# First graph layer of a four-layer graph transformer: x also loaded transposed, the layer-norm scale applied behind the projection, and the degrees split between two engines

## The reference, cut to what matters

```python
x = x + gnn0(layernorm(x), adj)      # sim = tanh(adj*adj) where adj > 0, top 350 of a row kept
                                     # h2 = tanh(layernorm(x) @ W_proj + b_proj)
                                     # feat = relu(new_adj @ (h2 @ W_gcn) + b_gcn)
x = x + moe0(layernorm(x))           # 8 experts, top 2, 128 -> 256 -> 128
x = x + gnn1(layernorm(x), adj)      # deg = row sums of adj + I; elu(D^-1/2 (adj+I) D^-1/2 x w)
x = x + block1(layernorm(x))         # attention and a second mixture of 8 experts
```

## Time and profile before

| what | value |
|---|---|
| median of 3 runs | 573.38 us (573.22 to 575.09) |
| the profiled execution's own time | 571.83 us |
| its span in the trace | 570.1 us |
| outside the span | 1.7 us |
| PE busy | 487.1 us, 85% |
| DVE busy | 427.9 us, 75% |
| ACT busy | 314.2 us, 55% |
| POOL busy | 252.3 us, 44% |

### The profile page before, as it was taken

One profiled execution on the slowest core, in us unless ns is written; L12 is line 12 of the kernel. 1 busy time (PEld: TensorE's weight loads), 2 busy tenths in 40 slices (PEclk: granted clock), 3 DMA queues, 4 the chain that ended last, 5 costly groups with the idle time before them and its releaser, 6 DMA issues.

```text
span 570.1 us, 11302 instructions
## 1 busy us (share of the span) xinstructions
PE 487.1 (85%) x3819; PEld 275.4 (48%) x3819; DVE 427.9 (75%) x1065; ACT 314.2 (55%) x522; POOL 252.3 (44%) x275
## 2 busy tenths in 40 slices
PE   1999995879999979998867778889989987898990
PEld 1533333557777745454432233233343226797990
DVE  6897966878999992565778679879977614866674
ACT  0687796966999900120113544456639654466770
POOL 3000002522444440110146189789946575377663
PEclk9999998989999999999957689999999996899996
DMA  8999975200115925011023443200040395869985
GB/s 293 400 422 423 421 274 178 93 1 22 30 28 203 409 58 115 0 42 28 15 75 99 122 118 104 90 2 1 0 143 20 135 356 160 250 182 361 399 299 186
DMA packets 39570, 93.43 MB, mean 164 GB/s; under 512 B 7488, under 2 KB 24944, under 8 KB 35168
## 3 DMA queue, kind: packets, MB, share of 16 engines
q1 hardware_dynamic: 35072, 86.96, 43.4%
q0 software_dynamic: 2272, 4.69, 2.3%
q10 hardware_dynamic: 2176, 1.13, 0.7%
HBM read 69.39 MB, written 21.00 MB: 159 GB/s over the span
## 4 chain that ended last, share of the span: by engine, by line
PE 54%; DVE 20%; DMA 9%; ACT 6%; issue 6%; SPq 3%; POOL 2%; POOLq 0%; DVEq 0%; ACTq 0%
PE ps L1586 9%; DVE A L2393 8%; PE ps L1763 8%; PE ps L1497 7%; PE ps L1514 6%; PE ps L1401 5%; PE ps L1755 3%; DMA R<-in_adj_in 3%; PE ps L1664 3%; DMA A<-w_split 2%; PE ps L1867 2%; PE ps L1611 2%; SPq L812 1%; PE ps L1381 1%; DMA slots_in<-R,A 1%
## 5 line engine op out<-in xcount | busy, mean ns | idle before, releaser
L2393 DVE TENSOR_REDUCE A<-ps 128x1 f32<-128x512 f32 (+3 forms) x160 | 86.1, 601 | 12.3 <-PE ps L1664 11.5
L1302 ACT ACTIVATE A<-ps 128x1024 f32<-128x1024 f32 (+3 forms) x80 | 68.4, 893 | 38.4 <-PE ps L1755 38.2
L1007 POOL TENSOR_TENSOR G<-G,A 128x1024 f32<-128x1024 f32 (+3 forms) x40 | 73.7, 1876 | 8.3 <-ACT A L1302 8.2
L1664 PE MATMUL ps<-A 96*128 96x512 f16 (+3 forms) x160 | 55.1, 382 | 10.3 <-DVE A L2393 4.5
L1401 PE MATMUL ps<-R,G 128*128 128x512 f32 x128 | 59.3, 605 | 1.2 <-DVE G L1967 0.8
L1586 PE MATMUL ps<-A,G 128*128 128x512 f32 x128 | 59.9, 594 | 0.0
L1514 PE MATMUL ps<-R 128*128 128x128 f16 x768 | 49.1, 221 | 7.0 <-DVE x L2085 5.8
L1514 PEld LDWEIGHTS ps<-R 128*128 128x128 f16 x768 | 46.1, 99 | 14.5 <-issue 6.6
L2067 DVE SCALAR_TENSOR_TENSOR R<-R 128x512 f16<-128x512 f32 x64 | 46.7, 752 | 6.8 <-ACT R L1157 6.5
L1867 PE MATMUL ps<-A 128*128 128x128 f16 (+1 forms) x702 | 47.6, 224 | 3.3 <-DMA A<-w_split 3.3
L1155 ACT ACTIVATE R<-ps,b 128x512 f32<-128x512 f32 x64 | 44.0, 688 | 10.6 <-PE ps L1497 9.4
(11 more groups left out here) (311 smaller groups left out, 920.7 us busy)
## 6 DMA issues: line engine op xcount, KB each, us to landing
A<-w_split SPq DMA_DIRECT2D x39, 533.0 KB, 10.2
A<-in_adj_t SPq DMA_DIRECT2D x16, 1024.0 KB, 17.6
slots_in<-xn SPq DMA_DIRECT2D x1, 8320.0 KB, 22.4
R<-in_adj_in SPq DMA_DIRECT2D x7, 1024.0 KB
w_split<-A SPq DMA_DIRECT2D x9, 725.0 KB, 4.0
xn<-in_adj_in SPq DMA_DIRECT2D x5, 1024.0 KB, 12.9
xT<-in_adj_in SPq DMA_DIRECT2D x4, 1024.0 KB, 12.6
A<-in_f_w SPq DMA_DIRECT2D x16, 170.5 KB
```

The lines of the kernel that those rows point to most:

```text
L1007: pool.tensor_tensor(total, total, probabilities(n, pair)[:, :, t0:CW], ALU.add).then_inc(s_sum, 1)
L1302: act.activation(probabilities(n, pair)[:, :, t0:CW], ps[:, 2 * pair:2 * pair + 2, t0:CW], ACT.Exp, scale=1.0 / (SQ * SQ * float(HD) ** 0. ...
L1664: last = pe.matmul(ps[:, bank, 0:width], queries(t // TPC, h)[0:KQ, P * (t % TPC):P * (t % TPC) + P], keys(b, h // (NH // NKV))[0:KQ, 0:wi ...
L2393: dve.reduce_max(pm[:, h, t % TPC, b:b + 1], ps[:, bank, 0:width], AX_X).then_inc(s_rmf, 1)
```

## The change

x is also given transposed (`x_t`) and loaded in four pieces into the third row buffer, between the adjacency tiles. The mean is taken out of the weights: PE multiplies W_proj by a 128 x 128 matrix of ones (`full_ones`, the memory of `comb`), DVE subtracts that product divided by 128 from W_proj. PE projects the raw transposed chunk (`projection`); DVE multiplies the product by the inverse root of each row and adds b_proj (`scaled_projection`), ACT applies tanh in place in `G` (`features_in`). W_gcn moves behind the aggregation: `features` only copies, and `features_back` multiplies by W_gcn, on top of a product of one row that adds b_gcn (`features_bias`); relu is joined to the addition to x. The statistics of chunks 2 and 3 and the scaling of chunks 1 to 3 stand between the squares on DVE; projection 3 stands behind the first aggregated tile on PE.

Only 8 of the 16 row tiles of adj are loaded and summed by ACT. For the other 8 PE sums the columns of the stored A tiles (`late_degrees`: per tile j four float32 products with 32 columns of ones and 256 columns of A each, in four column groups). DVE copies the sums, PE transposes them (`late_degrees_by_rows`), DVE adds 1.

```diff
-            ROWS_BEHIND = {3: (0,), 4: (1,), 6: (2,), 7: (3,), 9: (4,), 10: (5,), 12: (6,), 13: (7,), 15: (8, 9, 10, 11, 12, 13)}
+            ROWS_BEHIND = {4: (0,), 5: (1,), 6: (2,), 8: (3,), 10: (4,), 11: (5,), 13: (6,), 14: (7,)}
+            load_x(0)
+            load_x(1)
+            load_transposed_x(0)
             for j in range(NT):
                 sp.dma_start(A[:, j, :], adj_t[j]).then_inc(s_A[j], 16)
+                if j == 0:
+                    load_transposed_x(1)
+                    load_x(2)
+                if j == 1:
+                    load_transposed_x(2)
+                    load_x(3)
+                if j == 2:
+                    load_transposed_x(3)
                 for i in ROWS_BEHIND.get(j, ()):
                     load_rows(i)
...
-                act.activation(h2T[:, CW * g:CW * g + CW], ps[:, 4 + g, :], ACT.Tanh, bias=cols[:, 0:1]).then_inc(s_h2, 1)
+            def features_in(g):
+                act.wait_ge(s_h2, 1 + g + 1)
+                act.activation(flat0(G, slice(TPC * g, TPC * g + TPC)), flat0(G, slice(TPC * g, TPC * g + TPC)), ACT.Tanh).then_inc(s_G, 1)
...
-            SUMS_BEHIND = {0: (0,), 1: (1,), 3: (2,), 4: (3,), 6: (4,), 7: (5,), 9: (6,), 11: (7,), 13: (8,), 14: (9,),
-                           15: (10, 11, 12)}
+            SUMS_BEHIND = {4: (0,), 5: (1,), 6: (2,), 8: (3,), 10: (4,), 11: (5,), 13: (6,), 14: (7,)}
+            FEATURES_AHEAD = {0: 0, 3: 1, 7: 2, 11: 3}
...
+            pe.matmul(ps[:, 0, 0:P], full_ones, wmat[:, 0, :], start=True, stop=True).then_inc(s_h2p, 1)
+            def projection(g):
+                pe.wait_ge(s_xt[g], 16)
                 for q in range(TPC):
+                    last = pe.matmul(ps[:, 4 + g, P * q:P * q + P], raw_xT[:, P * (TPC * g + q):P * (TPC * g + q) + P], wmat[:, 0, :],
+                                     start=True, stop=True)
+                last.then_inc(s_h2p, 1)
+            pe.wait_ge(s_h2, 1)
+            for g in range(NC - 1):
+                projection(g)
...
-            pe.wait_ge(s_G, NC)
             for j in range(NT - 1):
+                if j == 1:
+                    projection(NC - 1)
+                if j % TPC == 0:
+                    pe.wait_ge(s_G, j // TPC + 1)
...
+            def features_bias(g):
+                pe.matmul(ps[:, 6 + g % 2, :], full_ones[0:1, :], gcn_bias[:, :].unsqueeze(1).broadcast_to([1, TPC, D]),
+                          start=True, stop=False, skip_group_check=True)
...
+            def late_degrees(tiles):
+                for j in tiles:
+                    for c in range(TPC):
+                        last = pe.matmul(ps[32 * c:32 * c + 32, DEGREE_BANK, 0:2 * P], ones[:, :], A[:, j, P * (ROWS + 2 * c):P * (ROWS + 2 * c + 2)],
+                                         start=(j == 0), stop=(j == NT - 1), skip_group_check=True)
+                return last
+            def late_degrees_by_rows():
+                pe.wait_ge(s_degr, 1)
+                for n in range(2):
+                    last = pe.transpose(ps[:, DEGREE_BANK, P * n:P * n + P], late_sums[:, P * n:P * n + P], ident[:, :])
+                last.then_inc(s_deg, 1)
             rows_back(2)
+            late_degrees(range(0, 2))
+            rows_back(3)
+            late_degrees(range(2, 4))
             rows_again(0)
-            rows_back(3)
-            rows_again(1)
+            late_degrees(range(4, 7))
...
                 hidden(0, gg)
-                if gg + 2 < NC:
-                    rows_again(gg + 2)
+                if gg == 0:
+                    rows_again(1)
+                    late_degrees(range(7, 10))
+                    rows_again(2)
+                if gg == 1:
+                    rows_again(3)
+                    late_degrees(range(10, 13))
+                if gg == 2:
+                    late_degrees(range(13, NT)).then_inc(s_deg, 1)
                 if gg == NC - 1:
                     output(0, 0)
                     output(0, 1)
                 elif gg >= NC:
                     output(0, gg - 2)
+                if gg == NC - 1:
+                    late_degrees_by_rows()
+                if gg == NC:
+                    pe.wait_ge(s_degr, 2)
...
+            AHEAD_OF = {3: ("scaled", 1), 6: ("stats", 2), 7: ("scaled", 2), 10: ("stats", 3), 11: ("scaled", 3)}
...
+                    if first and gg == NC - 1:
+                        dve.wait_ge(s_deg, 1)
+                        dve.tensor_copy(late_sums, ps[:, DEGREE_BANK, 0:2 * P]).then_inc(s_degr, 1)
```

More of the change, by code:

```diff
@@ L91, in loop_ends, with program @@
         self.base = self.done
-def program(nc, x_in, adj_t, adj_in, w_proj, b_proj, w_gcn, b_gcn, f0_wg, f0_bg, f0_bias, f0_w1, f0_b1,
+def program(nc, x_in, x_t, adj_t, adj_in, w_proj, b_proj, w_gcn, b_gcn, f0_wg, f0_bg, f0_bias, f0_w1, f0_b1,
             f0_w2, f0_b2, g1_w, ln1, ln2, wq, wk, wv, wo, w_router, f1_w1, f1_w2, f1_w3, cos_t, sin_t, out):
@@ L363, in program @@
         s_x = [sem(f"x_chunk{g}_loaded") for g in range(NC)]
+        s_xt = [sem(f"transposed_x_chunk{g}_loaded") for g in range(NC)]
         s_first = sem("first_operands_loaded")
@@ L409, in program @@
         s_relu = sem("hidden0_relu")
-        s_hhi = sem("hidden0_high")
         s_hlo = sem("hidden0_low")
@@ L1449, in _ @@
                 pe.wait_ge(g_feat, NC)
-                features_back(0)
-                features_back(1).then_inc(g_back, 1)
+                for g in range(2):
+                    features_bias(g)
+                    last = features_back(g)
+                last.then_inc(g_back, 1)
             def rows_back(g):
+                pe.wait_ge(s_x1, g - 1)
+                features_bias(g)
                 pe.wait_ge(s_feat, g + 1)
-                pe.wait_ge(s_x1, g - 1)
                 features_back(g).then_inc(s_ftr, 1)
@@ L1962, in mask @@
                 dve.tensor_scalar(mbuf[:, j % 2, :], fbuf[:, j % FB, :], 0.0, None, ALU.is_gt).then_inc(s_mask, 1)
+            row_statistics_in(0)
+            dve.wait_ge(s_first, 16 * len(first))
+            dve.wait_ge(s_h2p, 1)
+            dve.scalar_tensor_tensor(out=wmat[:, 0, :], in0=ps[:, 0, 0:P], scalar=-1.0 / D, in1=wmat[:, 0, :], op0=ALU.mult,
+                                     op1=ALU.add).then_inc(s_h2, 1)
+            row_statistics_in(1)
+            scaled_projection(0)
             square(0)
-            for g in range(NC):
-                dve.wait_ge(s_gp, g + 1)
-                dve.tensor_copy(rows(G, g), ps[:, g, :]).then_inc(s_G, 1)
+            AHEAD_OF = {3: ("scaled", 1), 6: ("stats", 2), 7: ("scaled", 2), 10: ("stats", 3), 11: ("scaled", 3)}
             for j in range(1, NT):
+                if j in AHEAD_OF:
+                    what, g = AHEAD_OF[j]
+                    if what == "stats":
+                        row_statistics_in(g)
+                    else:
+                        scaled_projection(g)
                 square(j)
@@ L2043, in _ @@
                     low_weights(w1l[:, 0], st_w1[:, 0], w1h[:, 0])
-            dve.wait_ge(s_rs, EARLY_ROWS)
+                dve.wait_ge(s_x1, g + 1)
+                statistics(g, x)
+            for b in range(3):
+                dve.wait_ge(s_rs[b], ROW_BUFFERS.count(b))
             for g in range(ON_SCALAR, NC):
@@ L2102, in turn @@
                 for gg in range(2 * NC):
+                    if first and gg == NC:
+                        dve.wait_ge(s_deg, 2)
+                        dve.tensor_scalar(sm[:, 11, ROWS:NT].rearrange("p (c s) -> p c s", s=2),
+                                          ps[:, DEGREE_BANK, 0:2 * P].rearrange("p (s c n) -> p c s n", s=2, c=TPC)[:, :, :, 0],
+                                          1.0, None, ALU.add).then_inc(s_degr, 1)
                     if not (first and gg == 2):
@@ L2138, in _ @@
             chain.loop_ends(E0 // 2 - 2, 2)
-            dve.wait_ge(s_rs, NT)
-            dve.tensor_scalar(sm[:, 11, :], sm[:, 11, :], 1.0, None, ALU.add).then_inc(s_degv, 1)
+            for b in range(3):
+                dve.wait_ge(s_rs[b], ROW_BUFFERS.count(b))
+            dve.tensor_scalar(sm[:, 11, 0:ROWS], sm[:, 11, 0:ROWS], 1.0, None, ALU.add).then_inc(s_degv, 1)
             turn(E0 // 2 - 1, False, True)
```

149 lines of the change are left out of this document (71 added, 78 removed).

## The result

The changed kernel takes 579.2 us (577.74 to 580.86, 6 runs); the kernel before took 573.38 beside it (572.79 to 576.49, 6 runs). The ratio is 1.009, 95% interval 1.0059 to 1.012: slower by 5 to 6 us, where 572.1 was forecast and 575.3 was the top of the range. The profiled execution took 579.68 us. Three of the ten executions of one experiment (two of the sixteen degree tiles) fell into a slower state of the chip and are left out of its median.

A forecast was written before the change was run, and what follows sets the result against it. PE was taken to bound the aggregation, waits and slow PE work the stage to the fourth gate, then DVE and PE. Terms -6.7 + 2.7 + 3.0 = -1.0 gave a median of 572.4, stated as 572.1 us; range 568.8 to 575.3.

The forecast's parts named there:

- Term 1: Start to end of aggregation: tile 0 starts at 15.5, aggregation ends at 81.3 us, -6.7 us.
- 3.9 MB are in at 13.6: Start: the loads up to the third transposed piece of x land by 13.6 us, so projection 2 ends at 15.5.
- the other path: Start: b_proj, weight correction, projection 0, scaling, then square and tanh on the way to tile 0, ending at 14.8 us.
- The slow rate in tile 0: Start of aggregation: PE's slow rate lasts until 17.7 us, so tile 0 loses 1.1 us.
- All of this I cost at nothing: Aggregation: supply of A and DVE's 6.4 us of added work cost no time, with 1.5 us of slack at tiles 11 to 15.
- Term 2: Aggregation end to fourth gate product: PE's added work makes it 22.3 us instead of 19.6, +2.7 us.
- at full rate: Aggregation end to fourth gate: PE, the bound throughout, runs at full rate, clock near 1.0.
- That it has one row of weights I take to change nothing: Behind the aggregation: a one-row b_gcn product costs 0.9 us like any float32 product of 512 columns, 3.6 for four.
- Term 3: Fourth gate to end of output(0,3): PE's late transposes wait for DVE's copy and hold up hidden(0,4), +3.0 us.
- Quick at the start: Rival, start: PE is quick, projections take 0.93 and tile 0 loses nothing; -2.0 us more, 570.1; chance 0.17.
- Starved: Rival, early start: first operand lands 1.7 us later or DVE falls behind; +1 to +2, about 573.6; chance 0.18.
- late degrees do run side by side: Rival claimed they do not, between aggregation and fourth gate: in series 29.6 us in place of 7.8, 594; chance 0.07.

The follow-up runs named there:

- two of the sixteen degree tiles: The changed kernel without the late degrees of tiles 1 to 14, 56 of 64 products left out; median 576.72 us, ratio 1.003.
- the degrees in the pause: Changed kernel with twelve of sixteen degree tiles moved behind hidden(0,3) and output(0,1), late transposes behind output(0,2); median 569.81 us, ratio 0.9908.

## Why the prediction was wrong

**Term 1, -6.7, measured -3.85.** Two steps failed. "3.9 MB are in at 13.6": the third piece landed at 16.9; nothing but SP's order kept it, since it came early when it was issued early. And the other path, put at 14.8, ended at 14.85 + 1.91 = 16.8: b_proj landed at 7.9, not 6.3, the first transposed piece at 9.4, not 7.5, and the tanh followed. The slow rate in tile 0 was right in size (0.95 for 1.1), projection 3 too. "All of this I cost at nothing" held for this kernel and fails from about 1 us earlier on: of the kernels that started earlier with the same loading of the row tiles, none ended the aggregation before 83.0, so the most that an early start was worth there is about 5 us.

**Term 2, +2.7, measured +5.8: the step that decided.** That PE would be the bound throughout was right, and "at full rate" was wrong. "That it has one row of weights I take to change nothing" was the false step: a row took 1.05 for 0.9, the products behind it 1.09 for 0.93, and the clock fell while PE was busy, 1.5 us here (25.38 against 23.84 with the clock at 1.00). By the chain, slow part included, the products with W_gcn took 5.3 for 3.7, the rows 4.3 for 3.6, the late degrees 8.3 for 7.8, and transposes, gates and `hidden` 7.6 for 6.8; the 0.4 for hand-overs wasn't needed. I had bounded the row from above by the 128-row product and left out what the change between the two costs.

I had read the slow `hidden(0,0)` of the earlier trace rows as the fruit of waiting. In that kernel PE did wait, 3.97 us up to 95.17, and the clock fell at 94.5, so it may be; but the Trainium skill (TensorE: Matmul & The Clock Gate, The HAM clock gate) ties the clock to how busy PE has been, and the trace agrees only in part: in the stretch from 89 to 96 above, PE was busy for 7.00 of 7.00 us at 0.56.

**Term 3, +3.0, measured +3.5.** Right in place, cause and nearly in size; moving the wait gave 3.6 back. What I missed is that `hidden(0,4)` would now pay the slow rate as well (2.56 for 1.3), less what came sooner behind it.

**Rivals.** "Quick at the start" didn't happen. "Starved" came in the form of its first condition, the late operand, at +2.8. The late degrees do run side by side. The range failed where a bound was no bound: it let a row of b_gcn be cheaper than the 128-row product and never dearer, and let the clock fall at the start only. The sum of the three terms' errors, 2.8 + 3.1 + 0.5 = 6.4, is the miss: 5.4 at the joints for the -1.0 forecast.

What stays open: why some traces with one-row products keep the clock, and what makes the part behind GNN1's start differ between executions. Of the five kernels with the degrees in the pause, the three without a slow stretch behind the aggregation have the lowest medians (567.01 to 568.68 against 569.59 and 569.81); that agrees with their joints, but the intervals don't resolve it.

## What to carry to other kernels

Before work is added to an engine in a stage where it waits, look for the longest pause behind it: fourteen degree tiles cost 5.8 us ahead of the fourth gate, twelve cost nothing behind it. A value that one engine hands over late should be asked for one step after the work that doesn't need it. A product of one row between full-height ones is not a cheap product here; spreading the operand over all partitions took 3.8 us out of the stage.

## What the runs showed of the hardware that was not expected

- Between full-height products, a float32 product of 512 columns took 1.05 us with one row of weights and 0.86 with 128; four float32 products of 128 columns behind it took 1.09 and 0.89. A second one-row product right behind the first took 0.86, so the surcharge lies at the change.
- PE's granted clock fell to 0.50, that is 1.2 GHz, while PE had been busy without a break, behind groups with one-row products (mean 0.56 from 89 to 96 us), and not behind the same groups with 128 rows (1.00).
- POOL's power of 128 x 4 elements took 3.3 us within the aggregation and 1.0 at the start: 

```profile
L908 POOL TENSOR_TENSOR roots<-variances,neg_half 128x4 f32<-128x4 f32 x2 | 6.7, 3328 | 38.8 <-DVE variances L1991 38.8
```
